# Two of four column groups of a graph layer by Strassen's scheme, with operand sums kept in DRAM

## The chip, the cores and the metric

The kernel runs on one NeuronCore of one Trainium2 chip. The metric is the device time of one execution in microseconds (us). Before the change it is 430.36 us, the median of three runs (428.66 to 430.53). The engines are called by the profile's names: PE is TensorE, DVE is VectorE, ACT is ScalarE, POOL is GpSimd, SP is the queue that issues the DMAs.

## The reference

The inputs are `x` (8 batches of 2048 x 128, f32), `adj` (2048 x 2048) and a weight `W` (128 x 128). Cut to what is computed:

```python
h = jnp.maximum(_layernorm(x, axis=-1), 0.0)
HW = jnp.einsum('bnf,fo->bno', h, W)
A_norm = jax.nn.relu((A + A.T) * 0.5)
D = jnp.sum(A_norm, axis=1)
d_inv_sqrt = jnp.where(D > 0, D_safe ** (-0.5), 0.0)
L_norm = jnp.eye(N) - d_inv_sqrt[:, None] * A_norm * d_inv_sqrt[None, :]
out = jnp.einsum('nm,bmo->bno', L_norm, HW)
return x + jax.nn.relu(out)
```

## The kernel before, in words

**Front.** `adj` is loaded in 16 squares of 512 x 512, turned on PE and added to itself on DVE, cut at zero on ACT (which sums the degrees) and mirrored. The result S stays in on-chip memory as 16 row blocks `mt` of 128 rows by 4 column groups `g` of 512 columns. Then the degrees' inverse roots are made.

**Precision by halves.** An f32 operand is used as two f16 numbers, a high and a low one. ACT writes the high half (`split_l_hi`, `split_h_hi`, `split_g_hi`), DVE the low half (`split_l_lo`, L407; `split_h_lo`, L384; `split_g_lo`, L412). A product of a pair of 128 x 128 by 128 x 512 blocks is three matmuls: high-high, high-low, low-high (L572 to L574). The halves of a piece of L lie in the place of that piece of S, its high half in the place that the piece before gave up; so `split_l_hi(t)` waits for `split_l_lo(t - 2)`.

**Stages.** The big product is done in 16 stages: four quarters (two batches each) by four column groups. A stage goes through the 16 row blocks in 16 slots `tau`; a slot is 2 batches by 3 matmuls. It fills two PSUM banks (two tiles `e`); six banks go round. A tile is then split into halves and multiplied with W (`multiply_w`, 12 small matmuls, in slots 3 and 5 of the next stage, `W_AT`). DVE cuts and scales the product (`take_product`, L420), POOL adds `x` (`add_x`, L286), SP stores it and loads the next `x` (`SUMS` buffers).

**What is made beside the stages.** In stages 0 and 1 PE waits in every slot for that slot's piece of L (`l_lo_ready`), which ACT and DVE make `LEAD` = 6 slots ahead in their programs. In stages 2 and 3 the same goes on without being needed at once. The normalised input comes in units `u` (a unit is 512 columns of h: two row blocks of two batches). DVE takes `statistics(u)` (L376, L379) in the slots of `stat_slot`; POOL's `normalise` handles two units at a time (a power, four small operations, then eight of 128x128, L268); ACT and DVE split the unit in the slot of `h_slot`. `statistics(u)` waits until unit u - 4 has been normalised (`xn_ready`), since `mv` has four slots. Each engine's program is written out slot by slot and each runs strictly in its order; nothing but semaphores ties the slots of one engine to those of another. Unit 8 is the first of the second quarter, unit 16 of the third.

## Time and profile before

| | |
|---|---|
| median of three runs | 430.36 us |
| the profiled execution's own time | 428.56 us |
| its span, first to last instruction | 426.8 us |
| mean granted clock of PE | 0.991 |
| PE busy | 394.8 us, 93% |
| DVE, POOL, ACT busy | 192.5, 181.1, 115.0 us |
| big matmuls, small matmuls with W | 1536, 384 |

The span is 1.8 us shorter than that execution's time. A big matmul is shown as 379 ns long although the next one starts after 216 ns, since they overlap in the array; so starts are to be compared, not durations.

### The profile page before, as it was taken

The numbers are of one execution on the slowest core, as the hardware profiler recorded it, in microseconds if no ns is written. First come the engines' busy times: TensorE is split into PE (matmuls) and PEld (weight loads), VectorE is DVE, ScalarE is ACT, GpSimd is POOL, SyncE is SP. The second block draws the span as 40 slices with busy tenths as digits, with TensorE's granted clock in tenths as the row PEclk, the third lists the DMA queues.
The fourth block names the chain that finished last, engine by engine and source line by source line (L and its number), as shares of the span: only waits on it lengthen the run. The fifth ranks groups of instructions, "written<-read, shape, count | busy, mean of one in ns | idle before, by whom it ended". The sixth has DMA issues, their size and how long they took to land.

```text
span 426.8 us, 5828 instructions
## 1 busy us (share of the span) xinstructions
PE 394.8 (93%) x2193; PEld 208.4 (49%) x2193; DVE 192.5 (45%) x519; ACT 115.0 (27%) x235; POOL 181.1 (42%) x295
## 2 busy tenths in 40 slices
PE   4648678999999999999999999999999999999994
PEld 3548653444444444454545454545454545454541
DVE  2697999979789844144614142431010202010211
ACT  1565986665657420102120102110100001010100
POOL 0088702077599957264955445813020111212211
PEclk9987999999999999999999999999999999999999
DMA  8999995103203343030022020031102020203011
GB/s 271 354 372 384 387 281 152 48 0 96 78 2 111 94 117 98 2 92 9 25 75 74 26 74 25 2 98 42 58 27 73 26 74 26 74 10 90 27 49 49
DMA packets 59820, 42.39 MB, mean 99 GB/s; under 512 B 2320, under 2 KB 51600, under 8 KB 59792
## 3 DMA queue, kind: packets, MB, share of 16 engines
q1 hardware_dynamic: 59792, 42.02, 31.8%
q8 instruction: 17, 0.28, 0.3%
q14 instruction: 11, 0.09, 0.1%
HBM read 33.62 MB, written 8.39 MB: 98 GB/s over the span
## 4 chain that ended last, share of the span: by engine, by line
PE 50%; issue 30%; POOL 7%; SPq 4%; DMA 3%; DVE 2%; ACT 2%; POOLq 0%
PE ps L572 14%; PE ps L573 14%; PE ps L574 14%; POOL sums L286 4%; DMA S<-in_adj_dram 3%; SPq L180 3%; PE ps L522 3%; PE ps L536 2%; POOL dsv L277 1%; SPq L195 1%; ACT S L316 1%; PE ps L586 1%; PE ps L587 1%; PE ps L588 1%; POOL xn L268 1%
## 5 line engine op out<-in xcount | busy, mean ns | idle before, releaser
L573 PE MATMUL ps<-S,hbuf 128*128 128x512 f16 x512 | 194.0, 379 | 0.0
L572 PE MATMUL ps<-S,hbuf 128*128 128x512 f16 x496 | 188.0, 379 | 0.0
L574 PE MATMUL ps<-S,hbuf 128*128 128x512 f16 x496 | 188.0, 379 | 0.0
L286 POOL TENSOR_TENSOR sums<-res,sums 128x512 f32<-128x512 f32 x32 | 42.8, 1343 | 160.9 <-DVE res L420 160.9
L573 PEld LDWEIGHTS ps<-S,hbuf 128*128 128x128 f16 x512 | 50.1, 98 | 56.5
L574 PEld LDWEIGHTS ps<-S,hbuf 128*128 128x128 f16 x496 | 48.5, 98 | 58.5
L572 PEld LDWEIGHTS ps<-S,hbuf 128*128 128x128 f16 x496 | 48.5, 98 | 54.9
L412 DVE SCALAR_TENSOR_TENSOR g<-ps,g 128x512 f16<-128x512 f32 x32 | 21.6, 686 | 114.5 <-ACT g L342 114.5
L342 ACT ACTIVATE g<-ps 128x512 f16<-128x512 f32 x32 | 19.0, 593 | 192.0 <-PE ps L574 191.5
L420 DVE SCALAR_TENSOR_TENSOR res<-ps,dsv 128x512 f32<-128x512 f32 x32 | 22.1, 689 | 75.8 <-PE ps L588 75.8
L336 ACT ACTIVATE S<-S,dneg 128x512 f16<-128x512 f32 x62 | 43.5, 719 | 21.6 <-DVE S L407 19.6
L407 DVE SCALAR_TENSOR_TENSOR S<-S,dneg 128x512 f16<-128x512 f32 x62 | 48.8, 808 | 1.1
L522 PE MATMUL ps<-ident,S 128*128 128x128 f32 x160 | 26.2, 333 | 18.2 <-DMA S<-in_adj_dram 12.2
L268 POOL TENSOR_SCALAR hbuf<-hbuf,lnt 128x128 f32<-128x128 f32 x64 | 35.2, 564 | 0.9
L522 PEld LDWEIGHTS ps<-ident,S 128*128 128x128 f32 x160 | 23.6, 175 | 20.2 <-issue 19.0
L249 POOL TENSOR_SCALAR lnt<-mv 128x8 f32<-128x8 f32 x16 | 6.7, 417 | 61.0 <-DVE mv L379 60.4
L316 ACT ACTIVATE S<-S 128x512 f32<-128x512 f32 x40 | 24.8, 621 | 22.1 <-DVE S L392 21.6
L392 DVE TENSOR_TENSOR S<-ps,S 128x512 f32<-128x512 f32 x40 | 25.4, 685 | 10.4 <-PE ps L522 10.4
L268 POOL TENSOR_SCALAR xn<-hbuf,lnt 128x128 f32<-128x128 f32 x64 | 29.3, 474 | 0.9
L252 POOL TENSOR_TENSOR lnt<-lnt,mhalf 128x8 f32<-128x8 f32 x16 | 27.8, 1737 | 0.0
L376 DVE BATCH_NORM_STATS2 stats<-hbuf 128x6 f32<-128x128 f32 x128 | 27.4, 276 | 0.0
L327 ACT ACTIVATE hbuf<-xn 128x512 f16<-128x512 f32 x16 | 9.9, 626 | 54.9 <-POOL xn L268 54.9
(69 smaller groups left out, 285.0 us busy)
## 6 DMA issues: line engine op xcount, KB each, us to landing
S<-in_adj_dram SPq DMA_DIRECT2D x16, 1024.0 KB, 12.4
hbuf<-in_x_dram SPq DMA_DIRECT2D x64, 128.0 KB, 3.5
sums<-in_x_dram SPq DMA_DIRECT2D x32, 256.0 KB, 2.8
out_dram<-sums SPq DMA_DIRECT2D x32, 256.0 KB, 2.6
res<-in_L_gnn_W_dram SPq DMA_DIRECT2D x1, 64.0 KB, 1.8
```

Of the source, the lines that this page charges most:

```text
L252: nc.gpsimd.tensor_tensor(y, v, mhalf[:], ALU.pow).then_inc(ln_chain, 1)
L268: last = nc.gpsimd.tensor_scalar(xn_buf(u, b, b + 1), x_buf(u, b, b + 1), neg_mean[:, c:c + 1], y[:, c:c + 1], ALU.add, ALU.mult)
L286: nc.gpsimd.tensor_tensor(sums[:, e % SUMS, :], res[:, e % 2, :], sums[:, e % SUMS, :], ALU.add).then_inc(sum_ready, 1)
L316: nc.scalar.activation(piece, piece, ACT.Relu, accum_out=deg_part[:, n, i:i + 1]).then_inc(s_ready, 1)
L336: nc.scalar.activation(l_hi(t), s_piece(t), ACT.Copy, scale=dneg[:, mt:mt + 1]).then_inc(l_hi_ready, 1)
L376: nc.vector.bn_stats(stats[:, u % 2, b, :], x_buf(u, b, b + 1)).then_inc(stats_raw, 1)
L392: nc.vector.tensor_tensor(piece, ps[:, k, :], piece, ALU.add).then_inc(a_added, 1)
L407: nc.vector.scalar_tensor_tensor(l_lo(t), s_piece(t), dneg[:, t % T:t % T + 1], l_hi(t), ALU.mult, ALU.subtract).then_inc(l_lo_ready, 1)
L522: last = nc.tensor.transpose(ps[:, k, q * P:(q + 1) * P], S[:, GRP * i + q, n * P:(n + 1) * P], ident[:])
L572: nc.tensor.matmul(acc, h_hi, l_hi(t), start=(mt == 0), stop=False)
L573: nc.tensor.matmul(acc, h_hi, l_lo(t), start=False, stop=False)
L574: last = nc.tensor.matmul(acc, h_lo, l_hi(t), start=False, stop=(mt == T - 1))
```

## The change

The first two column groups (0 and 1) are still done by plain stages: eight stages of 16 slots (`SLOTS` = 128). Groups 2 and 3 are done per quarter as one 2 by 2 block product: A is the two batches of h, each cut in the upper and lower 1024 rows; B is L's upper and lower half of group 2 and 3. The scheme needs seven half products (`ORDER`) for the eight of the plain way. A half product or part is 8 steps of 3 matmuls. It needs

- the sums of L's blocks T1, T2 and T4, which go to DRAM in halves (`t_forms`, `spill_form`) and come back into the place of groups 0 and 1 (`reload_form`) as soon as the plain stages have done with them, and T3, made in place. They are made on DVE in groups of four forms (`first_form` to `fourth_form`) every 10 slots from slot 33 (`form_slot`), each split by ACT and DVE, together with the four pieces of groups 2 and 3;
- the sums of h's blocks, per pair of units: `join_pair` (POOL), `combine_pair` (DVE, four operations), `split_pair_hi` (ACT), `split_pair_lo` (DVE);
- after the parts, seven sums in PSUM and on-chip memory on DVE per quarter (`sum_c11`, `sum_w`, `sum_c12` two, `sum_c22` two, `sum_c21`) and a copy on ACT (`copy_p1`).

A unit is now row blocks mt and mt + 8, so a quarter's eight units are all wanted in the first eight slots of its first stage. The second quarter's `h_slot` go from 16, 22, 28 ... 58 to 16, 18, 20 ... 30, its `statistics` from slots 8, 9, 20, 21 ... to 5, 6, 9, 10, 13, 14, 17, 18. The power on POOL is replaced by a root on ACT and a reciprocal on DVE for all units from 8 on; from unit 16 on ACT normalises and POOL makes the low half of h. `XN` goes from 2 to 1, `SUMS` from 3 to 2.

```diff
-W_AT = (3, 5)
+LN_STEPS = (1, 3, 4, 5)
+STAT_AHEAD = 11
+W_AT = (5, 7)
+ORDER = [1, 2, 6, 3, 5, 7, 4]
...
-    h_slot += [16 + 6 * k for k in range(UNITS)] + [68 + 6 * k for k in range(2 * UNITS)]
-    stat_slot += [h_slot[UNITS + k - k % LN_BATCH] - 8 + k % LN_BATCH for k in range(3 * UNITS)]
+    h_slot += [16, 18, 20, 22, 24, 26, 28, 30]
+    h_slot += [T * 2 + 1 + 4 * k for k in range(UNITS)] + [T * 4 + 1 + 4 * k for k in range(UNITS)]
+    stat_slot += [max(h_slot[UNITS + k - k % LN_BATCH] - STAT_AHEAD, 0) + k % LN_BATCH for k in range(3 * UNITS)]
+    form_slot = [33 + 10 * i for i in range(HALF)]
...
+            def first_form(i):
+                n = 3 * i
+                dve.wait_ge(b12_ready, i + 1)
+                if i:
+                    dve.wait_ge(t_out[0], 32 * i)
...
+            def sum_c21(q):
+                dve.wait_ge(part_done, len(ORDER) * (q + 1))
+                dve.wait_ge(u_ready, q + 1)
+                nc.vector.tensor_tensor(two(q, 4), two(q, 4), w_16, ALU.add).then_inc(c21_ready, 1)
...
+            for tau in range(SLOTS):
+                if tau - LN_STEPS[0] in pair_slot:
+                    normalise(pair_slot[tau - LN_STEPS[0]] * LN_BATCH)
+                if tau - LN_STEPS[3] in pair_slot:
+                    normalise(pair_slot[tau - LN_STEPS[3]] * LN_BATCH, 1)
...
+            take_product(TILES - 2)
+            sum_c21(QUARTERS - 1)
+            split_g_lo(TILES - 1)
+            take_product(TILES - 1)
...
-            for s in range(STAGES - 1):
+            for s in range(PLAIN):
...
+            for r in range(PARTS):
+                q, k = r // len(ORDER), r % len(ORDER)
+                e = PLAIN_TILES + 4 * q
+                wait_part(q, ORDER[k])
+                for i in range(HALF):
+                    if ORDER[k] in (3, 5, 6, 7) and i % 2 == 0:
+                        pe.wait_ge(s_lo_ready, UNITS // 2 * q + i // 2 + 1)
+                    part(q, ORDER[k], i)
```

**First place: DVE in stage 0, slots 10 to 14 of the program after.** L407 before is L768 after (`split_l_lo`), BN_STATS and BN_AGGR are `statistics`, and the number in `x_in8` is the unit's. Before, from slot 9 to the end of the stage:

```order
L376 BN_STATS stats<-hbuf 128x6 [waits xn_ready,x_in9]
L376 BN_STATS stats<-hbuf 128x6 x3
L379 BN_AGGR mv<-stats 128x2 [waits stats_raw] x4
L407 SCALAR_TENSOR_TENSOR S<-S,dneg 128x512 [waits l_hi_ready] x6
L412 SCALAR_TENSOR_TENSOR g<-ps,g 128x512 [waits g_hi_ready]
```

After:

```order
L728 BN_STATS stats<-hbuf 128x6 [waits xn_ready,x_in11]
L728 BN_STATS stats<-hbuf 128x6 x3
L731 BN_AGGR mv<-stats 128x2 [waits stats_raw] x4
L768 SCALAR_TENSOR_TENSOR S<-S,dneg 128x512 [waits l_hi_ready] x3
L728 BN_STATS stats<-hbuf 128x6 [waits xn_ready,x_in12]
L728 BN_STATS stats<-hbuf 128x6 x3
L731 BN_AGGR mv<-stats 128x2 [waits stats_raw] x4
L768 SCALAR_TENSOR_TENSOR S<-S,dneg 128x512 [waits l_hi_ready]
L737 RECIPROCAL lnt<-lnt 128x8 [waits ln_root]
L728 BN_STATS stats<-hbuf 128x6 [waits xn_ready,x_in13]
L728 BN_STATS stats<-hbuf 128x6 x3
L731 BN_AGGR mv<-stats 128x2 [waits stats_raw] x4
```

The statistics of units 11 to 13 (those of unit 10 stand just ahead) have moved between the pieces of L on which PE waits, and those of units 12 and 13 stand there with their wait on `xn_ready` (units 8 and 9).

**Second place: POOL at the start of the second quarter's normalisation.** L249, L250 and L252 before are a pair's first two operations and the power. Before:

```order
L249 TENSOR_SCALAR lnt<-mv 128x8 [waits stats_ready]
L250 TENSOR_SCALAR lnt<-mv 128x8
L252 TENSOR_TENSOR lnt<-lnt,mhalf 128x8 [waits ln_chain]
L254 TENSOR_TENSOR lnt<-lnt 128x8 [waits ln_chain]
L256 TENSOR_TENSOR lnt<-lnt 128x8 [waits ln_chain]
L258 TENSOR_SCALAR lnt<-lnt 128x8 [waits ln_chain]
L260 TENSOR_TENSOR lnt<-lnt 128x8 [waits ln_chain]
L268 TENSOR_SCALAR hbuf<-hbuf,lnt 128x128 [waits ln_chain]
L268 TENSOR_SCALAR hbuf<-hbuf,lnt 128x128 x7
```

After, from unit 8 on (L473 and L474 are L249 and L250; L497 is L268):

```order
L473 TENSOR_SCALAR lnt<-mv 128x8 [waits stats_ready]
L474 TENSOR_SCALAR lnt<-mv 128x8
L473 TENSOR_SCALAR lnt<-mv 128x8 [waits stats_ready]
L474 TENSOR_SCALAR lnt<-mv 128x8
L483 TENSOR_TENSOR lnt<-lnt 128x8 [waits ln_inverse]
L485 TENSOR_TENSOR lnt<-lnt 128x8 [waits ln_chain]
L487 TENSOR_SCALAR lnt<-lnt 128x8 [waits ln_chain]
L489 TENSOR_TENSOR lnt<-lnt 128x8 [waits ln_chain]
L497 TENSOR_SCALAR hbuf<-hbuf,lnt 128x128 [waits ln_chain]
L497 TENSOR_SCALAR hbuf<-hbuf,lnt 128x128 x7
```

The power is gone, and the first two operations of the next pair (units 10 and 11), which wait for that pair's statistics, stand ahead of the rest of units 8 and 9.

**Third place: DVE at the program's end.** Before:

```order
L412 SCALAR_TENSOR_TENSOR g<-ps,g 128x512 [waits g_hi_ready]
L420 SCALAR_TENSOR_TENSOR res<-ps,dsv 128x512 [waits sum_ready,dsv_ready,prod_done]
L412 SCALAR_TENSOR_TENSOR g<-ps,g 128x512 [waits g_hi_ready]
L420 SCALAR_TENSOR_TENSOR res<-ps,dsv 128x512 [waits sum_ready,dsv_ready,prod_done]
L74 UNCONDITIONAL_BRANCH
```

After (L876 is `split_g_lo`, L885 `take_product`, L872 `sum_c21`):

```order
L876 SCALAR_TENSOR_TENSOR g<-ps,g 128x512 [waits g_hi_ready]
L885 SCALAR_TENSOR_TENSOR res<-ps,dsv 128x512 [waits sum_ready,dsv_ready,prod_done] x2
L872 TENSOR_TENSOR ps<-ps,xn 128x512 [waits u_ready,part_done]
L876 SCALAR_TENSOR_TENSOR g<-ps,g 128x512 [waits g_hi_ready]
L885 SCALAR_TENSOR_TENSOR res<-ps,dsv 128x512 [waits sum_ready,dsv_ready,prod_done]
```

A sum now stands ahead of the last tile's split, and ahead of that sum `take_product` of the tile before.

## Rows read from the trace of the kernel before

**Rows 1.** The page: span; in 40 slices PE's clock (tenths) and DMA rate.

```profile
span 426.8 us, 5828 instructions
PEclk9987999999999999999999999999999999999999
...
GB/s 271 354 372 384 387 281 152 48 0 96 78 2 111 94 117 98 2 92 9 25 75 74 26 74 25 2 98 42 58 27 73 26 74 26 74 10 90 27 49 49
```

**Rows 2.** Busy time in three plain stages: PE, PEld, DVE, ACT, POOL, clock, DMA.

```profile
90.50:112.60 22.10, 22.10 (x122) 10.71 (x121) 16.84 (x37) 12.84 (x20) 17.38 (x25) 1.00 0.28 79
112.60:134.60 22.00, 22.00 (x121) 10.75 (x120) 19.91 (x55) 14.11 (x23) 16.00 (x20) 1.00 0.10 30
156.70:178.70 22.00, 22.00 (x121) 10.74 (x120) 6.76 (x23) 3.38 (x6) 13.06 (x25) 1.00 0.18 53
```

**Rows 3.** Timeline of PE, its stream's two ends: start, duration, instruction, [idle before <-releaser].

```profile
66.80 0.39 PE L572 MATMUL ps<-spare,hbuf 128*128 128x512 f16 x1 [1.65 <-DVE S L407]
...
68.51 0.39 PE L572 MATMUL ps<-spare,hbuf 128*128 128x512 f16 x1 [0.24 <-DVE S L407]
...
419.30 0.38 PE L574 MATMUL ps<-S,hbuf 128*128 128x512 f16 x1
421.10 0.23 PE L586 MATMUL ps<-w,g 128*128 128x128 f16 x1 [1.42 <-DVE g L412]
...
421.72 0.22 PE L588 MATMUL ps<-w,g 128*128 128x128 f16 x1
```

**Rows 4.** Groups by line and shape: count, busy us, mean ns, idle before.

```profile
L407 DVE SCALAR_TENSOR_TENSOR S<-S,dneg 128x512 f16<-128x512 f32 x62 | 48.8, 808 | 1.1
L286 POOL TENSOR_TENSOR sums<-res,sums 128x512 f32<-128x512 f32 x32 | 42.8, 1343 | 160.9 <-DVE res L420 160.9
L412 DVE SCALAR_TENSOR_TENSOR g<-ps,g 128x512 f16<-128x512 f32 x32 | 21.6, 686 | 114.5 <-ACT g L342 114.5
L384 DVE SCALAR_TENSOR_TENSOR hbuf<-hbuf 128x512 f16<-128x512 f32 x16 | 11.5, 736 | 8.5 <-ACT hbuf L327 8.5
```

**Rows 5.** Timeline of DVE in stage 0.

```profile
77.92 0.74 DVE L407 SCALAR_TENSOR_TENSOR S<-S,dneg 128x512 f16<-128x512 f32 x1
...
78.84 0.74 DVE L407 SCALAR_TENSOR_TENSOR S<-S,dneg 128x512 f16<-128x512 f32 x1
...
83.32 0.86 DVE L376 BATCH_NORM_STATS2 stats<-hbuf 128x6 f32<-128x128 f32 x4
...
84.38 4.46 DVE L407 SCALAR_TENSOR_TENSOR S<-S,dneg 128x512 f16<-128x512 f32 x6
```

**Rows 6.** Timeline of POOL: a pair normalised in the front, and one in stage 0.

```profile
31.19 3.45 POOL L268 TENSOR_SCALAR hbuf<-hbuf,lnt 128x128 f32<-128x128 f32 x8
...
84.55 0.60 POOL L249 TENSOR_SCALAR lnt<-mv 128x8 f32<-128x8 f32 x1 [16.91 <-DVE mv L379]
...
85.78 1.63 POOL L252 TENSOR_TENSOR lnt<-lnt,mhalf 128x8 f32<-128x8 f32 x1
87.48 0.75 POOL L254 TENSOR_TENSOR lnt<-lnt 128x8 f32<-128x8 f32 x1
...
89.58 4.27 POOL L268 TENSOR_SCALAR hbuf<-hbuf,lnt 128x128 f32<-128x128 f32 x8
```

**Rows 7.** Timeline of POOL in stage 1, one wide operation.

```profile
100.79 1.49 POOL L277 TENSOR_TENSOR dsv<-svec,dpos 128x512 f32<-128x512 f32 x1
```

**Rows 8.** Timeline of DVE over the same time.

```profile
101.30 1.52 DVE L384 SCALAR_TENSOR_TENSOR hbuf<-hbuf 128x512 f16<-128x512 f32 x1
```

**Rows 9.** The last tile, from DVE's and POOL's timelines.

```profile
420.35 0.69 DVE L412 SCALAR_TENSOR_TENSOR g<-ps,g 128x512 f16<-128x512 f32 x1 [6.41 <-ACT g L342]
421.98 0.69 DVE L420 SCALAR_TENSOR_TENSOR res<-ps,dsv 128x512 f32<-128x512 f32 x1 [0.94 <-PE ps L588]
422.75 1.26 POOL L286 TENSOR_TENSOR sums<-res,sums 128x512 f32<-128x512 f32 x1 [7.47 <-DVE res L420]
```

**Rows 10.** DMA issues: KB each, us to landing.

```profile
out_dram<-sums SPq DMA_DIRECT2D x32, 256.0 KB, 2.6
```

More of the change, by code:

```diff
@@ L89, in gnn_layer @@
         dsv = sb("dsv", [P, 2, WIDE])
+        form = sb("form", [P, FORM_SLOTS, WIDE])
+        form16 = form[:].bitcast(F16)
         ident = sb("ident", [P, P])
@@ new lines, in split_pair_hi @@
+            def split_pair_hi(n):
+                q, p = n // (UNITS // 2), n % (UNITS // 2)
+                act.wait_ge(s_chain, 4 * (n + 1))
+                if q:
+                    act.wait_ge(part_done, part_at(q - 1, 3) + 1)
+                else:
+                    act.wait_ge(acc_done, PLAIN_TILES - PAIR)
+                for a in range(2):
+                    last = nc.scalar.activation(a_home(q, a, 0, p), pair_buf(n)[:, :, 2 * a * P:2 * (a + 1) * P], ACT.Copy)
+                last.then_inc(s_hi_ready, 1)
@@ L357, in _ @@
                 split_l_hi(t)
-            for tau in range(T * STAGES):
+            for tau in range(SLOTS):
                 s = tau // T
@@ new lines, in _ @@
+                if tau - 2 in first_pair_slot:
+                    combine_pair(first_pair_slot.index(tau - 2))
+                if tau - 3 in first_pair_slot:
+                    split_pair_lo(first_pair_slot.index(tau - 3))
+            for r in range(PARTS):
+                q, k = r // len(ORDER), r % len(ORDER)
+                e = PLAIN_TILES + 4 * q
+                if r == 0:
+                    for c in (e - 2, e - 1):
+                        split_g_lo(c)
+                    for c in (e - 2, e - 1):
+                        take_product(c)
+                if q and k == 0:
+                    sum_c21(q - 1)
+                    split_g_lo(e - 1)
+                if k == 2:
+                    sum_c11(q)
+                if k == 3:
+                    sum_w(q)
+                if k == 5:
+                    sum_c12(q)
+                if k == 6:
+                    sum_c22(q)
+                if pair_in(r) is not None:
+                    combine_pair(pair_in(r))
+                if k in SUM_AT:
+                    split_g_lo(e + SUM_AT.index(k))
+                for c in taken_in(r):
+                    take_product(c)
+                if pair_in(r) is not None:
+                    split_pair_lo(pair_in(r))
```

573 lines of the change are left out of this document (480 added, 93 removed).

## The prediction

> **What bounds the kernel now.** I read the page first: the clock granted to PE is 0.7 and 0.8 in two slices of the front and full afterwards [rows 1]. Then PE's own timeline, by starts, since durations overlap. From 68.51 us, when the second slot of stage 0 begins, to the last big matmul at 419.30 no start comes late; the only idle times marked are 0.24 at the beginning and 1.42 at the end, where the last tile is split [rows 3]. Between these two starts lie 1529 big matmuls and 31 x 12 small ones. The small ones start every (421.72 - 421.10) / 11 = 0.056 us, so a big one costs (350.79 - 372 x 0.056) / 1529 = 0.2158 us. PE is therefore the bound for 350 of 427 us, and every big matmul less is worth its full 0.216 us as long as nothing makes PE wait. A slot is 1.295 us, a plain stage 96 x 0.2158 + 24 x 0.056 = 22.06 us.
>
> What stands close behind PE is seen in the stages' windows: DVE has 16.8 and 19.9 us of work in the 22 us of stages 1 and 2, and POOL 17.4 and 16.0, but DVE only 6.8 in a later stage [rows 2]. So the room is late in the kernel, and the change adds its work early.
>
> **What is removed.** The plain way does groups 2 and 3 in 8 x 96 = 768 big matmuls; the seven half products take 4 x 7 x 24 = 672. The 96 fewer give 96 x 0.2158 = **20.7 us**. The small ones stay 32 x 12. The power on POOL (1.63 us a pair, [rows 6]) is not on PE's path, since no wait of PE hung on it.
>
> **What is added at the end.** Before, from the last big start T = 419.30: that matmul ends at T + 0.38 and ACT splits, DVE splits at T + 1.05, the small matmuls start at T + 1.80, DVE at T + 2.68, POOL at T + 3.45, and the span ends at T + 7.5 [rows 1, 3, 9]. After, twelve small matmuls of tile 30 follow T, which moves T itself 0.7 earlier. But DVE has `take_product(30)` ahead of `sum_c21`, so it waits for them: it starts at T + 0.22 + 0.61 + 0.26 (the gap from the last small start to DVE, 421.72 to 421.98) = T + 1.1, takes 0.65, then the sum 0.7 (a PSUM operation of 128x512, as L412, [rows 4]), and the chain that began at T + 0.4 begins at T + 2.45: 2.0 later. With two `sums` buffers tile 31's `x` is loaded only after tile 29 is stored, 2.6 us to landing [rows 10] and the load about as much; I count another 0.2 for it. Net of the 0.7: **+1.5 us**. So without any new stall 428.56 - 20.7 + 1.5 = **409.4 us**, in the profiled execution's terms.
>
> **Stages 0 and 1, the first stall.** DVE needs 0.92 us for a piece of L with its diagonal and about 0.72 for the piece alone [rows 5], where PE uses one in 1.295. The 0.4 to 0.6 us of lead gained per slot is what the new schedule spends. Slot 5 of DVE starts at 77.92 [rows 5]. Slots 5 to 10 now hold 6 pieces (0.66 each), 4 diagonals (0.26), 4 units of statistics (1.06 each: 83.32 to 84.38, [rows 5]) and some small ones (0.4): 9.6 us, so unit 11's statistics end at 87.6. PE reaches slot 11 at 81.5 and slot 17 at 89.2, so this much is just covered.
>
> Then comes a ring. POOL waits with units 8 and 9 until unit 11's statistics are there, because the next pair's first two operations stand ahead. Its costs beside a busy DVE: 1.2 us for these two, 2.1 for the four small ones, 0.53 to 0.55 for each of the eight [rows 6]. So units 8 and 9 are ready at 93.1 and 95.3. DVE's statistics of unit 12 wait for unit 8, those of unit 13 for unit 9, and behind them on DVE stand pieces 20 and 21 of L, for which PE waits. Piece 21 comes at 95.3 + 1.06 + 0.7 = 97.1, and PE would want it at 94.4. Each later pair goes round the same ring: statistics 1.06, first two 1.2, four 2.1, eight 4.4 = 8.8 us, against PE's four slots = 5.2. With an idle DVE the eight take 3.45 [rows 6] and the small ones, by the same ratio, half: 6.0 us. DVE idles part of each round, so I take 8.1: units 11 and 13 at 103.4 and 111.5, unit 17's statistics at 112.6, then pieces 30 and 31 with a split of h between them (0.74, [rows 4]): 114.7. Slot 31 then ends at 116.0 instead of 109.9. **+6 us**, with bounds from the two ring times: at 8.8 it is 7.5; at 6.0 the ring is ahead of need and DVE's own added work alone makes piece 31 about 1 us late.
>
> **Stages 2 to 5, the second stall.** Nothing here is needed slot by slot, but PE waits in each stage's slot 5 for `split_g_lo` of the tile just finished, 5 slots and 12 matmuls after the stage's start, and that stands in DVE's queue behind the forms. I count DVE's program. Wide operations with two inputs on chip (forms, their low halves, low halves of L; nearest row L407, 0.67 to 0.81 us, [rows 4, 5]) number 16, 17, 19, 18, 18 in stages 2 to 6; at 0.74 that is 11.8, 12.6, 14.1, 13.3, 13.3 us. Four PSUM operations are 2.8 (L412, [rows 4]). Four statistics with their roots 4.7 in stages 2 to 4. Together 19.3, 20.1, 21.6, then 16 and 16. Added to it is what POOL's wide operations cost DVE: in stage 1 DVE's split of h took 1.52 us instead of its mean 0.74 while POOL's L277 ran from 100.79 to 102.28 [rows 4, 7, 8]. POOL now has six such per stage (four low halves of h, two `add_x`, 1.3 us each, [rows 4]). Each can cost DVE from nothing to 0.8 us; I take half, 2.4 us a stage. That makes 21.7, 22.5 and 24.0 us in stages 2 to 4 against 22.06, and DVE comes into stage 2 late: unit 15 is normalised at 117.5 (two units after 113); POOL then has 1.2 for a next pair, two `add_x` 2.7 and five small ones 2.6, so unit 16's scale is there at 124, ACT needs it ahead of its six operations up to the first form's operand (some 2.5 us), and DVE's forms of slot 35 wait for that until about 127, 7 us behind PE's slot 35 at 120. Going on by these costs, `split_g_lo` of tiles 4, 6 and 8 ends 2, 1 and 2 us after PE wants it. **+4 us** (5, less what DVE gains where POOL is idle), from 0 (0.67 an operation, no collisions) to 9 (every collision full).
>
> The rule of the Trainium skill (SBUF — State Buffer, section "Who interferes with whom") is that a DVE instruction with two SBUF inputs and a GpSimd instruction that reads SBUF exclude each other, and the later one stands still until the other has ended. The trace agrees: 102.28 + 0.74 is 103.0, and DVE's operation ended at 102.82. By the rule, were DVE always the later one by a little, its stages 2 to 4 would be some 2.5 us longer each than I take, which lies in rival B.
>
> **Costed at nothing.** The spilled forms (6.3 MB out, 6.3 back): form 1 returns during stage 7, form 0 has four parts (21 us) and form 2 six (31 us) before it is read. A form is 2 MB: 5.4 us at the front's 387 GB/s [rows 1], 21 us at the 256 KB in 2.6 us of a single store [rows 10]. Only near the slow end would form 2 come late, by up to 10 us; its rows of 1 KB are between those of the two, and with 16 queues full I take the fast end. The sums in the parts: a quarter of 28 x 24 matmuls and its W steps is 39 us, DVE has 7 sums, 8 PSUM operations and 4 pairs, under 20 us. The tightest is tile 1 of a quarter: two sums, four operations on a pair and the split, about 4.1 us, where PE asks after 5.8; 1.7 us of room, four times. The first eight units are wanted by slot 7 (76.3 us), and DVE's slot 1, behind the last two of them, starts four times 0.92 before 77.92, at 74.2 [rows 5].
>
> **Sum.** 409.4 + 6 + 4 = 419.4 us as the profiled execution counts; that one (428.56) was below the median of the runs by 1.8, so for the median I say **420 us**.
>
> **Rivals.** (A) *No stall*: the ring turns at its fast 6.0 us and POOL and DVE rarely meet. For it: in stage 2 DVE had 19.9 us of work and POOL 16.0 [rows 2] without a late start of PE. Against it: the ring's rows with a busy DVE. Time 409 to 413. (B) *DVE becomes the bound in stages 2 to 5*: 24 to 25 us a stage against 22.06, together about 9 instead of 4, time 424 to 428. For it: the count above, and that ACT and DVE wait for each other at every half of a form. Against: in stages 5 and 6 there are 6 us of room to recover. (C) *Slower than before*: the same place and mechanism, but worse. The gain left after the ring is 13 us; it is gone when DVE's program in stages 2 to 5 takes 22.06 + 13 / 4 = 25.3 us a stage, which the count reaches only if all six collisions cost 0.8 (+2.5) and each form's ping-pong with ACT leaves DVE idle for over 1 us. Then 431 to 437. (D) *The gate on PE's clock*: the half clock (1.2 GHz) appears only in the front, after long idle; an idle time of 1.65 us before the first product [rows 3] did not bring it, and the ring's stalls are 1 to 2 us each. If it fell for a while in stage 1, each big matmul there would cost twice 0.216, 6 us for 27 of them; time 424 to 427. It is counted with B.
>
> **Numbers.** Forecast (one stall in stage 1, a smaller one behind, 413 to 424): 0.60. A: 0.16. B with D: 0.13. C: 0.07; between B and C, within 0.5% of before: 0.04. The range of 8 in 10 leaves out C and the ends of A: 410 to 427. Half a percent, about what a measurement of this kernel can tell from no change, is 2.2 us: faster 0.87, same 0.05, slower 0.08.
>
> **What would show it.** Big matmuls 1440. In stage 1, DVE idle before BN_STATS, released by POOL, and PE idle before L1087 to L1089, released by the low half of L, some 6 us in all. In stages 3 to 5, PE idle before L1130 (the W step) released by `split_g_lo`. Stages 6 and 7 at 22.06 us and the parts at 5.2 us each plus W, without waits. DVE's last `take_product` of tile 30 ahead of the sum. Wrong would be: stage 1 of 22 us; waits of PE in the parts; half clock in the stages; a wait on the forms from DRAM.

## The result: 1.7% slower

The changed kernel takes **436.53 us**, the median of four runs (435.52 to 440.23), against 430.05 for the kernel before, run beside it (four runs, 428.66 to 430.53). The ratio is 1.017, with a 95% interval of 1.011 to 1.024. The forecast was 420 us and faster; the time lies above its range.

The profiled execution took 435.52 us, the shortest of the four, and had the highest mean clock of them, 0.968 against 0.956 to 0.963; so what its trace shows of the clock is rather too little. Its page, to be read beside [rows 1] (span, busy times, and PE's clock in tenths over forty slices of 10.8 us):

```profile
span 433.7 us, 6127 instructions
PE 379.2 (87%) x2097; PEld 198.4 (46%) x2097; DVE 309.9 (71%) x696; ACT 178.1 (41%) x379; POOL 185.0 (43%) x247
PEclk9877999999999999998999997999999999999998
```

PE's busy time fell from 394.8 to 379.2 us, DVE's rose from 192.5 to 309.9, and ACT's from 115.0 to 178.1. PE's clock, full in every slice behind the front before, is below it twice. PE's stream has 1440 big matmuls and runs from 66.91 to 424.26, 357.4 us; before, 1536 took 352.5 [rows 3]. So 20.7 us of matmuls went and PE stood for longer than that. These are the main ones of the starts that come late, with the last start ahead of the three largest waits (PE's timeline; start, duration, instruction, idle before and releaser):

```profile
94.05 0.39 PE L1087 MATMUL ps<-S,hbuf 128*128 128x512 f16 x1 [0.65 <-DVE S L768]
...
102.88 0.39 PE L1087 MATMUL ps<-S,hbuf 128*128 128x512 f16 x1 [1.22 <-DVE S L768]
...
105.61 0.39 PE L1087 MATMUL ps<-S,hbuf 128*128 128x512 f16 x1 [1.26 <-DVE S L768]
...
113.19 0.39 PE L1087 MATMUL ps<-S,hbuf 128*128 128x512 f16 x1 [2.23 <-DVE S L768]
...
126.96 0.23 PE L1130 MATMUL ps<-w,g 128*128 128x128 f16 x1 [0.94 <-DVE g L876]
...
193.90 0.38 PE L1089 MATMUL ps<-S,hbuf 128*128 128x512 f16 x1
197.79 0.29 PE L1130 MATMUL ps<-w,g 128*128 128x128 f16 x1 [3.51 <-DVE g L876]
...
261.50 0.38 PE L1101 MATMUL ps<-S,hbuf 128*128 128x512 f16 x1
267.45 0.29 PE L1130 MATMUL ps<-w,g 128*128 128x128 f16 x1 [5.57 <-DVE g L876]
...
300.85 0.23 PE L1130 MATMUL ps<-w,g 128*128 128x128 f16 x1 [0.77 <-DVE g L876]
...
424.26 0.38 PE L1101 MATMUL ps<-S,hbuf 128*128 128x512 f16 x1
...
428.06 0.23 PE L1130 MATMUL ps<-w,g 128*128 128x128 f16 x1 [2.75 <-DVE g L876]
```

How late a start is, I work out as its distance to the start before, less 0.216 us (0.2158) behind a big matmul and 0.056 behind a small one. Summed to the last big start this gives 26.7 us, of which 0.4 stood there before:

| where | what PE waits for | late, us | forecast |
|---|---|---|---|
| stages 0 and 1, six times | low half of L (L768) | 7.9 | 6 |
| stages 2, 3 and 5, W step of tiles 2, 4, 8 | `split_g_lo` (L876) | 1.1 + 0.9 + 3.7 | 4 |
| behind tile 8's wait | half clock | 1.7 | 0 |
| first part, W step of tile 14 | `split_g_lo` | 5.7 | 0 |
| behind it | half clock | 2.6 | 0 |
| later parts, W steps | `split_g_lo`; at some the trace shows no releaser | 2.5: one of 0.9, five of 0.3 | 0 |

The end behind T, the last big start, takes 9.5 us; the forecast's terms give 7.5 + 2.0 + 0.2 = 9.7. So the loss is three groups of waits of nearly equal size, 7.9, 7.4 and 8.3 us.

What DVE did at three of these places, in the ring (92 to 102), ahead of tile 8's W step (186 to 198) and ahead of tile 14's (240 to 268), is in its timeline:

```profile
92.20 0.87 DVE L728 BATCH_NORM_STATS2 stats<-hbuf 128x6 f32<-128x128 f32 x4 [2.58 <-POOL hbuf L497]
...
93.27 0.72 DVE L768 SCALAR_TENSOR_TENSOR S<-S,dneg 128x512 f16<-128x512 f32 x1
...
101.03 0.87 DVE L728 BATCH_NORM_STATS2 stats<-hbuf 128x6 f32<-128x128 f32 x4 [1.71 <-POOL hbuf L497]
...
186.47 1.38 DVE L780 SCALAR_TENSOR_TENSOR form<-S,npos 128x512 f32<-128x512 f32 x1
187.89 1.53 DVE L790 SCALAR_TENSOR_TENSOR S<-S,dneg 128x512 f32<-128x512 f32 x1
189.34 1.75 DVE L800 SCALAR_TENSOR_TENSOR form<-S,dneg,form 128x512 f32<-128x512 f32 x1
...
197.05 0.68 DVE L876 SCALAR_TENSOR_TENSOR g<-ps,g 128x512 f16<-128x512 f32 x1
...
240.82 2.33 DVE L823 TENSOR_TENSOR form<-form 128x256 f32<-128x256 f32 x1 [3.52 <-POOL form L540]
243.18 0.42 DVE L825 TENSOR_TENSOR form<-form 128x256 f32<-128x256 f32 x1
...
265.50 1.29 DVE L835 TENSOR_TENSOR S<-form,spare 128x512 f16<-128x512 f32 x2 [1.21 <-ACT spare L648]
266.71 1.28 DVE L876 SCALAR_TENSOR_TENSOR g<-ps,g 128x512 f16<-128x512 f32 x2
```

And POOL's timeline over the same stretches:

```profile
90.36 3.94 POOL L497 TENSOR_SCALAR hbuf<-hbuf,lnt 128x128 f32<-128x128 f32 x8
...
98.80 4.86 POOL L497 TENSOR_SCALAR hbuf<-hbuf,lnt 128x128 f32<-128x128 f32 x8
...
187.26 1.61 POOL L503 TENSOR_TENSOR hbuf<-xn,hbuf 128x512 f16<-128x512 f32 x1
188.83 1.71 POOL L519 TENSOR_TENSOR sums<-res,sums 128x512 f32<-128x512 f32 x1
...
238.67 4.20 POOL L540 TENSOR_TENSOR form<-hbuf 128x1024 f32<-128x1024 f16 x2 [10.58 <-DMA t_forms<-form]
247.21 2.12 POOL L540 TENSOR_TENSOR form<-hbuf 128x1024 f32<-128x1024 f16 x1 [4.34 <-DVE S L835]
```

**The ring** is there as described: DVE's statistics wait for POOL's normalised units, and a piece of L stands behind them. One round takes 8.4 us (90.36 to 98.80) where PE's four slots take 5.2. **The collisions in stages 2 to 5** are seen at 186 to 191: three wide operations of DVE, which alone take about 0.75, take 1.38 to 1.75 while POOL's wide ones run, and the split of tile 8 comes at 197.05, 3 us behind PE's last start.

**The first part** is what the forecast did not have. POOL's first sum of blocks of h starts at 238.67, after a spill of a form has landed. DVE's first operation on it is stretched by POOL's second sum from 0.42 to 2.33 us; pair by pair DVE's four operations, ACT's split and DVE's split follow each other, with the ends at 247.0, 254.4, 262.6 and 266.8, and the split of tile 14 stands behind the fourth. The second and third pair take 7.4 and 8.1 us while POOL makes the sums of the pairs behind them and adds `x`; the fourth, with POOL idle, takes 4.2. (In the longer two stands a `take_product` of 0.7.) What was issued late stands in SP's own timeline (the duration is the time that SP took for the issue):

```profile
231.62 0.45 SPq L374 DMA_DIRECT2D out_dram<-sums  x1
234.04 0.38 SPq L368 DMA_DIRECT2D sums<-in_x_dram  x1
234.53 1.11 SPq L407 DMA_DIRECT2D t_forms<-form  x1
...
236.65 0.45 SPq L408 DMA_DIRECT2D t_forms<-form  x1
...
262.31 0.45 SPq L416 DMA_DIRECT2D S<-t_forms  x1
...
265.21 3.07 SPq L420 DMA_DIRECT2D S<-t_forms  x1
```

The last forms' spills are queued behind a tile's store and the load that waits for its landing (231.62 to 234.04), and go out by 236.65; 2.0 us later POOL starts. The reload of form 1 is issued at 262.31, behind the results of all plain tiles but two. Four of the reloads hold SP itself for 1.7 to 3.1 us each, and the `x` of later tiles stands behind them.

**The clock.** Four windows; the columns are length, busy us (and instructions) of PE, PEld, DVE, ACT, POOL, granted clock, DMA share and GB/s:

```profile
198.00:202.00 4.00, 4.00 (x21) 2.20 (x20) 3.59 (x7) 3.35 (x9) 1.45 (x2) 0.60 0.19 66
202.00:206.00 4.00, 4.00 (x29) 2.18 (x28) 3.75 (x6) 3.10 (x7) 3.67 (x6) 1.00 0.00 0
...
266.00:270.00 4.00, 2.55 (x16) 1.73 (x17) 2.68 (x5) 0.43 (x1) 0.28 (x1) 0.50 1.06 350
270.00:274.00 4.00, 4.00 (x23) 2.37 (x22) 0.69 (x1) 0.60 (x1) 1.42 (x2) 0.64 1.10 350
```

Behind the idle times of 3.51 and 5.57 us PE runs at its lower level, 1.2 GHz, for 3.4 and 5.4 us; a big matmul starts every 0.43 us there. Behind 2.23 us (at 113.19) it does not in this execution; the experiments show the same idle time with the half clock behind it.

### The profile page after: what moved, and what is told of

Same layout as the page of the kernel before. It is cut to its first block, busy times and chain, and to the rows that moved or that the text cites. A ratio compares the mean times of both kernels' runs of the same rounds, so it can differ in the third digit from the quotient of the medians.

```text
span 433.7 us, 6127 instructions
## 1 busy us (share of the span) xinstructions
PE 379.2 (87%) x2097; PEld 198.4 (46%) x2097; DVE 309.9 (71%) x696; ACT 178.1 (41%) x379; POOL 185.0 (43%) x247
## 4 chain that ended last, share of the span: by engine, by line
DVE 25%; issue 24%; POOL 17%; DMA 14%; PE 9%; SPq 5%; ACT 5%; POOLq 0%; DVEq 0%; ACTq 0%
DMA out_dram<-sums 7%; POOL form L540 5%; DMA sums<-in_x_dram 4%; POOL hbuf L497 4%; POOL sums L519 4%; DVE form L823 3%; DVE S L768 3%; SPq L363 3%; DMA S<-in_adj_dram 2%; DVE stats L728 2%; PE ps L1087 2%; PE ps L1088 2%; PE ps L1089 2%; DVE S L749 2%; DVE form L815 1%
## 5 line engine op out<-in xcount | busy, mean ns | idle before, releaser
L1087 PE MATMUL ps<-S,hbuf 128*128 128x512 f16 x240 | 91.5, 381 | 6.9 <-DVE S L768 6.9
L1088 PE MATMUL ps<-S,hbuf 128*128 128x512 f16 x256 | 97.5, 381 | 0.0
L519 POOL TENSOR_TENSOR sums<-res,sums 128x512 f32<-128x512 f32 x32 | 46.8, 1462 | 117.1 <-DVE res L885 106.3
L1089 PE MATMUL ps<-S,hbuf 128*128 128x512 f16 x240 | 91.2, 380 | 0.0
L1099 PE MATMUL ps<-S,hbuf 128*128 128x512 f16 x160 | 61.3, 383 | 0.0
L1100 PE MATMUL ps<-S,hbuf 128*128 128x512 f16 x160 | 61.2, 382 | 0.0
L1101 PE MATMUL ps<-S,hbuf 128*128 128x512 f16 x160 | 61.1, 382 | 0.0
L540 POOL TENSOR_TENSOR form<-hbuf 128x1024 f32<-128x1024 f16 x16 | 35.1, 2205 | 31.8 <-DVE S L835 16.9
L621 ACT ACTIVATE S<-S,dneg 128x512 f16<-128x512 f32 x54 | 37.7, 714 | 18.9 <-DVE S L768 17.0
L1037 PE MATMUL ps<-ident,S 128*128 128x128 f32 x160 | 24.4, 318 | 20.1 <-issue 12.0
L768 DVE SCALAR_TENSOR_TENSOR S<-S,dneg 128x512 f16<-128x512 f32 x54 | 41.5, 776 | 0.1
L1087 PEld LDWEIGHTS ps<-S,hbuf 128*128 128x128 f16 x240 | 23.6, 98 | 36.2 <-DVE S L768 10.1
L1130 PE MATMUL ps<-w,g 128*128 128x128 f16 x128 | 24.7, 228 | 15.1 <-DVE g L876 14.8
L1088 PEld LDWEIGHTS ps<-S,hbuf 128*128 128x128 f16 x256 | 25.2, 98 | 27.7 <-issue 0.3
L1089 PEld LDWEIGHTS ps<-S,hbuf 128*128 128x128 f16 x240 | 23.6, 98 | 28.7 <-issue 0.6
L648 ACT ACTIVATE hbuf<-form 128x512 f16<-128x512 f32 x16 | 9.6, 625 | 58.8 <-DVE form L829 58.8
L497 POOL TENSOR_SCALAR hbuf<-hbuf,lnt 128x128 f32<-128x128 f32 x64 | 33.1, 531 | 0.9
L749 DVE TENSOR_TENSOR S<-ps,S 128x512 f32<-128x512 f32 x40 | 25.3, 683 | 10.3 <-PE ps L1037 10.2
L885 DVE SCALAR_TENSOR_TENSOR res<-ps,dsv 128x512 f32<-128x512 f32 x32 | 21.9, 683 | 15.0 <-PE ps L1132 15.0
```

The costliest lines, as they stand in the source:

```text
L497: last = nc.gpsimd.tensor_scalar(xn_buf(u, b, b + 1), x_buf(u, b, b + 1), neg_mean[:, c:c + 1], y[:, c:c + 1], ALU.add, ALU.mult)
L519: nc.gpsimd.tensor_tensor(sums[:, e % SUMS, :], res[:, e % 2, :], sums[:, e % SUMS, :], ALU.add).then_inc(sum_ready, 1)
L540: nc.gpsimd.tensor_tensor(pair_buf(n), hbuf[:, u:u + 2, 0, :], hbuf[:, u:u + 2, 1, :], ALU.add).then_inc(pair_ready, 1)
L621: nc.scalar.activation(l_hi(t), s_piece(t), ACT.Copy, scale=dneg[:, mt:mt + 1]).then_inc(l_hi_ready, 1)
L768: nc.vector.scalar_tensor_tensor(l_lo(t), s_piece(t), dneg[:, mt:mt + 1], l_hi(t), ALU.mult, ALU.subtract).then_inc(l_lo_ready, 1)
L1087: nc.tensor.matmul(acc, h_hi, l_hi(t), start=(mt == 0), stop=False)
```

## The experiments

The theory after the result: four chains of other engines hold PE in turn, (1) the ring, (2) DVE's work with POOL's collisions, seen by the W step in slot 5, (3) the pairs ahead of the split of tile 14, (4) SP's order. The W steps placed later are the repair of (2); they were not tried alone, only together with others. Two rivals: that one of them, above all the first, is the cause and the others follow from it; and that the idle times matter mainly by the half clock. To take the front's scatter out (the first big matmul starts anywhere from 66.8 to 68.8), I compare traces by the time from the first big matmul to the span's end, "stream to end", and note when tile 14's W step starts after that first matmul, where PE waits for it. All results, times as medians, ratios to the kernel before in the same call:

| kernel | us | ratio, 95% interval | stream to end | W step of 14 |
|---|---|---|---|---|
| before | 430.05 | 1 | 360.0 | |
| the change | 436.53 | 1.017 (1.011 to 1.024) | 366.8 | 200.5 |
| ring only | 435.91 | 1.018 (1.012 to 1.023) | 365.1 | 198.1 |
| pairs only | 439.81 | 1.023 (1.020 to 1.027) | 368.4 | no wait |
| fillers | 437.15 | 1.018 (1.016 to 1.021) | 367.3 | 200.9 |
| SP's order only | 433.59 | 1.010 (1.006 to 1.013) | 363.3 | 200.2 |
| no low half of h | 430.91 | 1.004 (1.003 to 1.006) | 363.4 | 195.9 |
| SP's order, late W | 425.20 | 0.989 (0.987 to 0.992) | 355.3 | 192.5 |
| ring, pairs, late W | 434.71 | 1.011 (1.007 to 1.015) | 362.8 | no wait |
| **all four** | **414.21** | **0.963 (0.961 to 0.966)** | **344.7** | no wait |
| all but the ring | 419.26 | 0.977 (0.975 to 0.979) | 349.3 | no wait |
| all but the pairs | 420.69 | 0.981 (0.978 to 0.984) | 352.0 | 189.4 |
| all but late W | 424.11 | 0.988 (0.984 to 0.992) | 352.9 | no wait |
| all four, h later | 416.95 | 0.972 (0.969 to 0.974) | 347.1 | no wait |

### The ring alone

```diff
-LN_SLOTS = 4
+LN_SLOTS = 8
```

DVE's statistics of unit u then wait for unit u - 8.

> mv gets eight slots instead of four, so statistics(u) waits for unit u - 8 and no longer stands in DVE's queue behind POOL; nothing else is changed. Theory 1 (each stall has its own place and cause): PE's lateness in stages 0 and 1, 8.0 us in the changed kernel, falls to 1 to 2 us, DVE shows no idle before BN_STATS released by POOL, and the run is 4 to 7 us faster than the changed kernel, about 430. Theory 2 (DVE's and POOL's work in the plain stages is the bound, so a stall that is removed comes back behind it): stage 1 is repaired, but the waits for the low half of tiles 2 to 8 grow by about as much, and the run stays within 2 us of the changed kernel.

Stages 0 and 1 came out 3.3 us late (three waits, 1.21, 1.05 and 0.99) instead of 7.9, so the ring was the cause of 4.6 us there. The waits left are not DVE's own work alone: DVE stood idle for ACT for 0.93 and 1.17 us (up to 102.67 and 106.02), and ACT just before for POOL's normalisation for 2.34 and 1.92 us. The time hardly followed: 0.6 us by the medians, within the intervals, 1.7 in the traces. Tile 2's W step, 1.1 late in the change, is 2.9 late here, with the half clock behind it, and tile 14's is still 5.7 late. PE came to tile 2's W step 4.5 us earlier, but DVE's half of it was ready only 2.6 us earlier; most of the gain was given back to such waits and to the clock. Neither expectation came out whole.

### The pairs alone

`combine_pair` and the splits of pairs 2 and 3 go behind the splits of tiles 14 and 15, on ACT and on DVE:

```diff
-                if tau - 2 in first_pair_slot:
+                if tau - 2 in first_pair_slot[:2]:
                     combine_pair(first_pair_slot.index(tau - 2))
...
                     for c in (e - 2, e - 1):
                         split_g_lo(c)
+                    for n in (2, 3):
+                        combine_pair(n)
+                        split_pair_lo(n)
                     for c in (e - 2, e - 1):
                         take_product(c)
```

> Pairs 2 and 3 of the first quarter's sums of h are combined and split behind the splits of tiles 14 and 15 instead of ahead of them, on ACT and DVE. Theory 1: the wait of 5.6 us before the W step in the first part goes, and with it the half clock behind it (2.6 us); pairs 2 and 3 are still in time for the third part. 7 to 8 us faster than the changed kernel, about 429. Theory 2: the pairs are now late for the third part, and PE waits there for as long, within 2 us of the changed kernel.

The wait at tile 14's W step is gone, and yet nothing is won: 3.3 us more than the change by the medians, with intervals that overlap, and 1.6 more in the traces. PE now reaches the third part before form 1 is back from DRAM (1.4 us late), and a W step of the first quarter's parts is 8.1 us late, with the half clock behind it. Its `split_g_lo` stands on DVE behind a pair of the second quarter, whose join stands on POOL behind an `add_x` that waited 14.95 us for its `x`; that load SP could issue only at 284.99, when a store that was queued behind the reloads had landed.

### Fillers against the half clock

Ten and sixteen matmuls of no use into the product's bank, ahead of the wait for tiles 8 and 14:

```diff
+                for i in range({8: 10, 14: 16}.get(e, 0)):
+                    nc.tensor.matmul(ps[:, 6 + e % 2, :], hbuf[:, 0, 0, 0:P], hbuf[:, 0, 0, :], start=True, stop=True)
                 pe.wait_ge(g_lo_ready, e + 1)
```

> Ahead of the W steps of tiles 8 and 14, where PE stood idle for 3.5 and 5.6 us, PE does 10 and 16 matmuls into the bank that the step is about to overwrite (2.2 and 3.5 us), so that the idle time left is about 1.3 and 2.1 us. If the half clock behind these two waits (1.7 us and 2.6 us in the changed kernel) comes from PE's idling, it goes, and the run is about 4 us faster although it does 26 matmuls more. If it comes from something else (the whole activity, DMA), the granted clock stays half there and the run is as long as the changed kernel or up to 1 us longer.

The wait for `prod_taken`, which frees that bank, moves ahead of the fillers. The idle times left were 1.62 and 3.48 us. Behind the first the half clock was gone (1.67 us late in the change, 0.05 here), behind the second it stayed for a part (1.5 instead of 2.6), and the mean clock rose from 0.968 to 0.977. The time did not fall: what was won behind tile 8 was waited for at tile 14, whose W step starts 200.9 us after the first matmul (200.5 in the change). Of the 1.1 us won behind tile 14, 0.4 went at the next late W step, and the end took 0.7 more, since tile 31's small matmuls ran at the half clock. The rival that the clock is the main loss falls.

### SP's order alone

The results of tiles 10 and 11 go behind the last spills, the reload of form 1 behind them at the start of stage 7 (it stood behind tile 13), and the results of tiles 14 and 15 ahead of form 2's reload:

```diff
-                if tau >= T and tau % T in STORE_AT:
+                if tau >= T and tau % T in STORE_AT and tau // T != 6:
...
+                if tau == 6 * T + T:
+                    result(10)
+                    result(11)
+                    sp.wait_ge(acc_done, PLAIN_TILES - PAIR)
+                    reload_form(1)
-            sp.wait_ge(acc_done, PLAIN_TILES - PAIR)
-            reload_form(1)
             sp.wait_ge(acc_done, PLAIN_TILES)
             reload_form(0)
+            result(PLAIN_TILES - 2)
+            result(PLAIN_TILES - 1)
             reload_form(2)
-            for e in range(PLAIN_TILES - PAIR, TILES):
+            for e in range(PLAIN_TILES, TILES):
                 result(e)
```

> Only SP's order is changed: the two results of stage 6 stand behind the last spilled form instead of ahead of it, form 1 is brought back at the start of stage 7 instead of behind the results of that stage, and form 2 behind the results of tiles 14 and 15. Theory SP (the order of SP's queue holds the first parts back: in the changed kernel POOL's first sum of a pair waited 10.6 us for the last spill, and add_x of tile 16 waited 10.8 us for its x behind the reloads): the first sum starts 2 to 3 us earlier, the wait before tile 14's W step falls from 5.6 to about 3, the 1 to 1.5 us wait of the next W steps goes, form 1 is never late; 431 to 433. Theory DVE (the pairs' own chain on POOL, DVE and ACT, 5 to 8 us a pair, is the bound there): within 1.5 us of the changed kernel.

It gave 2.9 us (3.5 in the trace), a little less than the 3.5 to 5.5 expected: no half clock follows tile 14's wait, which is 3.75 instead of 5.73, and the later W step is 0.3 late instead of 0.9. Tile 14's W step itself comes hardly earlier (200.2); the wait is shorter because tile 8's cost more here (4.1 and 2.8 of half clock).

### No low half of h from unit 16 on

```diff
-                nc.gpsimd.tensor_tensor(hbuf[:, u, 1, :], xn_buf(u), hbuf[:, u, 0, :], ALU.subtract).then_inc(h_lo2_ready, 1)
+                nc.gpsimd.memset(hbuf[:, u, 1, :], 0.0).then_inc(h_lo2_ready, 1)
```

This leaves out the low halves of h in the last two quarters; matmuls and waits stay.

> POOL's low half of h from unit 16 on is replaced by zeros written to the same place (that part of the product is left out of the last two quarters), so POOL reads nothing there while DVE makes the forms. Theory collisions (two-input DVE operations stand still behind POOL's reading operations): the forms' operations of 1.2 to 1.8 us return to 0.75, DVE gains 5 to 10 us over stages 2 to 5, the wait of 3.5 us before tile 8's W step goes with its half clock, 430 to 433. If collisions are minor: DVE's group means stay and the run is within 1.5 us of the changed kernel.

Stages 2 to 5 had no late W step at all; with the half clock behind tile 8, 7.4 us went. From 115 to 240 us DVE's wide operations became shorter (means of L768 from 0.82 to 0.74 us, of L815 from 0.86 to 0.79, of L800 from 0.87 to 0.75), 5.7 us in all. So these waits come from POOL's subtraction. That it is DVE being held up is what the shorter operations speak for; POOL's own program also became 11.6 us shorter there (16 operations in 8.4 instead of 20.0 us), and this run does not part the two.

Of the 7.4 us only 3.4 reached the end (366.8 to 363.4). Tile 14's W step is 5.5 late, as before, and a later one 2.1 instead of 0.9. The rest is the clock: the waits of stages 0 and 1 are the same, but the half clock follows the one of 2.23 us here and not in the change, which costs 2.8 us. PE's timeline and two windows of this kernel, and as the last row the first of these windows in the change:

```profile
113.23 0.39 PE L1087 MATMUL ps<-S,hbuf 128*128 128x512 f16 x1 [2.23 <-DVE S L768]
```

```profile
114.00:118.00 4.00, 3.23 (x10) 0.98 (x8) 2.76 (x10) 0.00 (x0) 3.79 (x7) 0.56 0.14 43
118.00:122.00 4.00, 4.00 (x12) 1.50 (x11) 1.00 (x2) 1.76 (x5) 3.83 (x8) 0.58 0.09 25
114.00:118.00 4.00, 3.17 (x16) 1.20 (x14) 2.72 (x10) 0.00 (x0) 3.81 (x7) 1.00 0.15 44
```

### Three of them together

The ring, the pairs, and the W steps later in the stage (and in the second part instead of the first), with the additions and stores behind them; at the end of the program the sum goes ahead of `take_product(30)`. This last edit is in all kernels below except the one with SP's order and late W steps; in the traces it makes the end 0.9 to 1.1 us shorter.

```diff
-W_AT = (5, 7)
-ADD_AT = (8, 10)
-STORE_AT = (11, 13)
+W_AT = (10, 12)
+ADD_AT = (13, 15)
+STORE_AT = (14, 15)
...
-            take_product(TILES - 2)
             sum_c21(QUARTERS - 1)
+            take_product(TILES - 2)
             split_g_lo(TILES - 1)
...
-                    if r == 0 and i in W_AT:
-                        multiply_w(e - 2 + W_AT.index(i))
+                    if r == 1 and i in (0, 2):
+                        multiply_w(PLAIN_TILES - 2 + i // 2)
```

> Eight slots of mv, pairs 2 and 3 behind the splits, the W steps of a plain stage in slots 10 and 12 instead of 5 and 7 (of the last plain stage in the second part), and at the end sum_c21 ahead of the take_product of tile 30. Theory 1: 96 matmuls are saved and all but 2 to 5 us of the stalls go: 411 to 417, faster than before the change by 3 to 4%. Theory 2: DVE's work of about 20 us a stage with POOL's collisions holds PE back elsewhere: 425 to 431.

PE ran from the first slot to the third part with 3 us of lateness in all. Then it stood for longer than in any kernel so far (PE's timeline):

```profile
267.08 0.59 PE L1104 MATMUL ps<-S 128*128 128x512 f16 x1 [9.59 <-issue]
...
296.78 0.29 PE L1135 MATMUL ps<-w,g 128*128 128x128 f16 x1 [4.88 <-DVE g L878]
```

The first is the wait for form 1. "issue" says that the profile shows no event for it, but SP issued its reload at 257.91 and 258.41, a reload takes 9.5 us to land on the page, and 267.08 is 8.7 after the second issue. The other wait, 4.88 us, has the same chain as in the kernel with the pairs alone, and begins on POOL (its timeline):

```profile
282.58 1.27 POOL L519 TENSOR_TENSOR sums<-res,sums 128x512 f32<-128x512 f32 x1 [16.93 <-DMA sums<-in_x_dram]
```

Its `x` was issued at 279.60, when the store of 270.10 had landed. Three repairs had moved the bound to the fourth chain: these two waits are 14.8 us late, and the half clock behind them costs 4.0; the trace is 18.1 us longer than with all four. The expectation, that all but 2 to 5 us of the stalls would go, failed.

### All four

The kernel above with SP's order.

> The kernel of e4_all with SP's order of e7_sp. In e4_all PE waited 9.6 us before the third part for form 1, which SP issued only at 257.9, and 4.9 us in quarter 0's last part behind POOL's add_x, which waited 16.9 us for its x behind the reloads. Theory SP: both waits go, with the half clock behind them (about 3.5 us): 411 to 417, faster than before the change by 3 to 4%. Theory DVE: the pairs are late for the third part by about as much: 423 to 430.

**414.21 us**, 3.7% below the kernel before (interval 3.4 to 3.9%) and the best of the study. Its page, and its only waits of 0.5 us or more between the start of stage 0's second slot and the end:

```profile
span 413.5 us, 6123 instructions
PE 377.2 (91%) x2097; PEld 198.4 (48%) x2097; DVE 301.5 (73%) x696; ACT 178.1 (43%) x379; POOL 184.6 (45%) x247
PEclk9696998999999999999999999999999999999998
```

```profile
102.57 0.39 PE L1097 MATMUL ps<-S,hbuf 128*128 128x512 f16 x1 [0.79 <-DVE S L775]
108.26 0.39 PE L1097 MATMUL ps<-S,hbuf 128*128 128x512 f16 x1 [0.97 <-DVE S L775]
...
407.51 0.23 PE L1140 MATMUL ps<-w,g 128*128 128x128 f16 x1 [1.48 <-DVE g L883]
```

The clock is full from the front to the last big matmul. The reload of form 1 is issued at 235.00 instead of 262.31, and the lateness up to the last big matmul is 5.5 us instead of 26.7: 0.4 at the start, 2.9 in stages 0 and 1, and 2.1 in six W steps of the parts.

### One left out at a time

SP's order with the late W steps alone, and the best version without the ring's slots, without the pairs' move, and with the early W steps:

> SP's order of e7_sp and the W steps in slots 10 and 12 (of the last plain stage in the second part); statistics, pairs and end as in the changed kernel. Theory SP plus late W: the waits before the W steps of tiles 2, 4, 8 and 14 (1.1, 0.9, 3.7, 5.7 us late) go, the 8 us of stages 0 and 1 stay: 419 to 424. If DVE's work is the bound in the plain stages: 428 or more.

> The best kernel so far (e8_all_sp, 414.2) with mv back at four slots. Theory 1 (with SP's order and the W steps out of the way, what PE loses in a stage is lost in the end): 5 us slower, about 419, since the 8 us of stages 0 and 1 come back where e8_all_sp has 3. Theory 2 (the later chain of forms and pairs sets the end, so an early stall is absorbed, as in e1_ring): 416 or less.

> e8_all_sp with pairs 2 and 3 of the first quarter back ahead of the splits of tiles 14 and 15. In e9_sp_latew PE stood 3.3 us before the W step of tile 14 with this order. Theory 1: 3 to 5 us slower, 417 to 419. If the earlier spill and the W step in the second part already give enough room: within 1 us of e8_all_sp.

> e8_all_sp with the W steps back in slots 5 and 7. Theory 1: the waits for the low half of tiles 2, 4 and 8 come back (2.9 and 3.4 us late in e1_ring, with half clock behind the longer), 6 to 9 us slower, 420 to 423. Theory 2: 416 or less.

Two of the four chains repaired already gave 425.2. From the best version, the ring costs 5.0 us (stages 0 and 1 are 7.8 late against 2.9), the pairs 6.5 (tile 14's W step 5.0 late and the half clock behind it), the early W steps 9.9 and SP's order 20.5 (434.71 against 414.21). Since these are medians of different calls, the ratios to the kernel before are the better measure: by them it is 5.8, 7.5, 10.5 and 20.3 us, and in the traces 4.6, 7.3, 8.2 and 18.1. The ring cost what was expected, the pairs and the W steps more than the 3 to 5 and 6 to 9 us written down. Against the change itself the ring gave 0.6, SP's order 2.9, and the pairs took 3.3 (medians of different calls; for the ring and the pairs the intervals overlap that of the change). Without the late W steps tile 2 and tile 8 are 3.0 and 3.2 late, and the half clock behind tile 2 costs 1.7 (PE's timeline of that kernel):

```profile
124.32 0.23 PE L1140 MATMUL ps<-w,g 128*128 128x128 f16 x1 [2.81 <-DVE g L883]
...
195.41 0.23 PE L1140 MATMUL ps<-w,g 128*128 128x128 f16 x1 [3.05 <-DVE g L883]
```

### The units of the second quarter later

The best version with `h_slot` of units 8 to 15 at 17, 20, 23, 25, 27, 29, 31, 32 while their statistics stay.

```diff
-    h_slot += [16, 18, 20, 22, 24, 26, 28, 30]
+    stat_of = [16, 18, 20, 22, 24, 26, 28, 30]
+    h_slot += [17, 20, 23, 25, 27, 29, 31, 32]
```

> e8_all_sp with the splits of units 8 to 15 of h in slots 17, 20, 23, 25, 27, 29, 31, 32 instead of 16, 18 ... 30 (their statistics stay where they are). In e8_all_sp ACT and DVE stood before these splits for POOL, which takes 8.0 us a pair, with the pieces of L behind them, and PE was 3 us late. If that is the cause: 1 to 2.5 us faster than e8_all_sp, 411.5 to 413. If DVE's own work in stage 1 is the cause: no difference.

Stages 0 and 1 were hardly better (2.8 against 2.9), and stage 2 got three new waits for the units themselves, 0.8, 1.06 and 0.93 us late. Both expectations were wrong. It is 2.7 us slower than the best version; the intervals of the ratios do not touch.

## Why the prediction was wrong

**What PE saves: right.** 1440 big matmuls, one every 0.216 us.

**The end of the program: right.** 9.5 us behind the last big start for 9.7. With the sum ahead of `take_product(30)` tile 31's split makes PE 1.6 late instead of 2.9.

**The ring: right in place and mechanism, small in size.** 7.9 us against 6 (the upper bound was 7.5). A round took 8.4 to 9.8 us (POOL's eight begin at 90.4 and 98.8, the pairs' last statistics at 94.4, 103.8 and 113.6) against the 8.1 taken. Removing it removed 4.6 us of waits and left 3.3, where the lower bound had 1 for DVE's own added work. POOL's normalisation, for which ACT and through it DVE stood, has a part in these: its eight operations took up to 6.6 us there, with DVE hardly idle, where the ring's slow bound had 4.4.

**Stages 2 to 5: right in place and mechanism, small in size.** 5.7 us of waits against 4, and 1.7 of half clock. Tiles 4 and 8 were named with 2 and 2 us and had 0.9 and 3.7; the 1 us named for tile 6 did not appear, and tile 2 had 1.1. The prediction took half of 0.8 us for each meeting of DVE and POOL; the three at 186 to 191 cost 0.6 to 1.0 each. Taking POOL's subtraction away removed all these waits.

**The step that failed is "Costed at nothing".** It held the forms' way through DRAM and the work in the parts for free, and priced the transfers by bandwidth and the sums by DVE's busy time. Neither was the price. What came late was the *issue* (the prediction had form 1 return during stage 7, and SP issued that reload at 262.31, behind the stage's last start at 261.50), because SP's queue has the results of tiles, each with its wait for POOL, ahead of spills and reloads. And the first quarter's four pairs were not in the count as a chain: 0.42 us an operation, but a round of DVE, ACT and DVE of 4.2 us when POOL is idle and of 7.4 to 8.1 us when it is not, with the split of tile 14 behind the fourth. The part "tile 1 of a quarter" looked at later quarters and not at the entry into the first. In the change it cost 5.7 + 2.6 us at tile 14. The W steps of the parts behind it were 2.5 late, of which 2.1 stand in the best version too, where the forecast had none. Taken back from the best version, SP's order alone cost 20 us and the pairs 6.5 to 7.5.

**The clock (rival D) was weighed too low.** It was argued from an idle time of 1.65 us that had not brought the half clock, and from stalls of 1 to 2 us. The stalls of 3.5 and 5.6 us did bring it, 4.3 us in all. And the place that the rival named, stage 1, had it in four other kernels: behind idle times of 2.03 (SP's order with late W steps) and 2.23 us (pairs only, fillers, no low half of h), for 3.4 to 6.8 us. That is a price on top of the waits and not their cause: where fillers took a part of it away, the time stayed.

**Rival C had the time (431 to 437) but not the mechanism.** It put all the loss into stages 2 to 5 at 25.3 us a stage. They lost 7.4 us with the clock, 1.9 a stage.

**What the sum could not show.** The forecast added the stalls. They do not add. Tile 14's W step starts 200.9 us after the first matmul with the fillers, 200.5 in the change and 200.2 with SP's order, while PE was 14.3, 15.4 and 17.0 us late up to there: the other engines' programs set this time, not how late PE comes, so what PE wins earlier it waits for here. Without the ring these programs themselves are earlier there, and the step starts at 198.1. Together the four repairs, with the sum at the end, give 22.3 us. The sum without any stall was 409.4, in the profiled execution's terms; the best version's profiled execution took 415.32 and has 5.5 us of lateness. So the scheme's gain is real and was lost in the order of the other engines' programs. Of the 2.9 us left in stages 0 and 1, how much is DVE's work and how much POOL's slow normalisation stays open: h's splits placed later moved the waits into stage 2, where PE then waited for the units, and did not remove them.

## What to carry to other kernels

Where work is taken from the engine that is the bound and put on others, follow each in-order queue, the DMA queue first, through the place where one phase meets the next, and ask of every late item what stands ahead of it there; bandwidth and busy shares say nothing on it. When several chains hold the bound engine in turn, a repair made alone can show next to nothing, as the ring and the pairs did, so repair all that the trace names and then take them back one at a time. Place a wait of the bound engine as late as its buffers allow: moving the W step by five slots, with the additions and stores behind it, was worth 8 us in the traces and 10 by the medians.
